# The gathers of a deformable convolution as one stream of quads: loads spread over a set, the fold behind the row sums, five broadcasts behind the fold

## The chip, the cores and the metric

The kernel runs on one core of one Trainium2 chip. The metric is the device time of one execution in microseconds. Before the change it is 5976.82 us, the median of 3 runs (5971.12 to 5979.78).

## What is computed

The reference applies four layers to an image batch x of shape 8 x 256 x 32 x 32 in float32, each with a normalisation before it and a residual behind it. The third holds three deformable convolutions, and these concern the change. Each computes offsets by a 3 x 3 convolution and then reads every pixel of every channel at its own fractional position:

```python
def _deform(x, ow, ob):
    off = _conv(x, ow, 1) + ob[None, :, None, None]
    off = off.reshape(B, C, 2, H, W)
    py = jnp.clip(yy + off[:, :, 0], 0.0, H - 1)
    px = jnp.clip(xx + off[:, :, 1], 0.0, W - 1)
    ...
    return v00 * (1 - wy) * (1 - wx) + v01 * (1 - wy) * wx + v10 * wy * (1 - wx) + v11 * wy * wx

x = x + _L0_conv_ref(_gn(x), ...)   # selective scan
x = x + _L1_conv_ref(_gn(x), ...)   # mixture of experts
x = x + _L2_conv_ref(_gn(x), ...)   # three deformable convolutions
x = x + _L3_conv_ref(_gn(x), ...)   # channel mixing
```

`_deform` runs on 256, 64 and 64 channels.

## The kernel before, in words

`kernel_program` builds the stages one after the other, each a block (or a hardware loop of blocks) with a barrier behind it: the scan layer, the expert layer, `build_offsets_1` (offsets of the first deformable convolution, 2 turns of 4 images), the constants, then `build_gather` "g1", `build_middle` 2, gather "g2", `build_middle` 3, gather "g3", and `build_last`. The stages hand data on through tensors in DRAM: `dense` (the image's second differences, called steps), `coords` (positions, y and x, in a high and a low part), `whole` (the y positions), `gathered`.

**The gather without an index.** A bilinear sample at (y, x) is a sum over all rows and columns of second differences, weighted with a clamped ramp in y and one in x. For four channels at a time (a *quad*) and half an image (512 pixels) a gather does, with n the number of the quad:

- *Broadcast* (line 1457, TensorE): a matmul with a 0/1 matrix `spread` copies a position row to 32 partitions in one of three PSUM banks, used as a ring. Each quad has five: four for x (`v`) and one for y (`k`, channel 0 of the quad). The other three y rows come by DMA (`send_rows`, line 1346), broadcast from `whole` to 32 partitions each, into `rows`, three buffers deep.
- *Read* (line 1401, ScalarE): the ramp's lower clamp, from the ring to `kw` or `vw`. It frees the bank (`ring_read`). VectorE does the same for the three sent rows (line 1423, `relu`), and GpSimd applies the upper clamp to all four (line 1415).
- *Row sums* (line 1472, TensorE): 16 matmuls on 32 x 32 tiles, image times `kw`, into four PSUM banks of one buffer only.
- *Weigh* (line 1434, VectorE): two products with `vw`, from those four banks to `prod`. It must end before the next quad's row sums start.
- *Fold* (line 1482, TensorE): four matmuls that sum 32 partitions, accumulated in one bank over the eight quads of a half. Then ScalarE copies that bank to `res` (line 1386, `evacuate`) and SyncE stores it.

A *set* is 128 channels: two halves of eight quads, 16 quads. g1 has 16 sets, g2 and g3 have 4. A hardware loop runs turns of `SETS` = 4 sets, 64 quads unrolled; coordinates and images have a buffer for each of the four sets, and semaphores are cleared between turns. The order on TensorE is written out:

```python
for n in range(-2, Q):
    tasks = turn_tasks(n)          # v, v, v of quad n+1, k of quad n+2, last v of n+1
    if n >= 0:
        rows_step(n)
    for task in tasks[:3]:
        spread_step(task)
    if n >= 1:
        fold_step(n - 1)
    for task in tasks[3:]:
        spread_step(task)
```

A broadcast waits for the read of the one three before it. ScalarE reads in the same order and evacuates behind its five reads of every eighth quad; the first fold of the next half waits for that (`res_ready`). All transfers are issued by SyncE, in program order: the first quad's rows, `load_set(0)`, two more quads' rows, `load_set(1)` to `load_set(3)`, then rows for quad n as soon as VectorE has read those of quad n-3. A `load_set` is four coordinate transfers of 512 KB (128 partitions) and four image transfers (128 KB each), which read `dense` in runs of 32 elements (128 bytes).

The producers of `dense` are `build_offsets_1` (line 1219, SyncE, in an image's first quarter) and `build_middle` (line 1638, one store per image ahead of that image's coordinates).

Of the kernel before, what the change touches and what calls it, by code (L numbers as in the profile page):

```python
# [32 lines left out]
SETS = 4  # L33
# [1115 lines left out]
def build_offsets_1(nc, t, ps, xcur, dense, coords, whole):  # L1149

    with ExitStack() as ctx:
# [54 lines left out]
        with nc.Fori(0, B // IMGS) as turn:  # L1206
            b0 = turn * IMGS
            with nc.Block() as block:

                @block.sync  # L1210
                def _(sp):
                    for m in range(2):
                        sp.dma_start(x[:, m], image(xcur, b0 + m)).then_inc(sem(f"x_loaded{m}"), 16)
                    for i, (m, k, y) in enumerate(kinds):
                        if k == 0 and y == 0:

                            sp.wait_ge(sem("steps_ready"), KC * (m + 1))
                            sp.dma_start(dense[bass.ds((b0 + m) * C, C), :].rearrange("(k p) n -> p k n", p=P),
                                         x[:, m % 2]).then_inc(sem(f"stored{m}"), 16)
                            if m + 2 < IMGS:  # L1220
                                sp.wait_ge(sem(f"stored{m}"), 16)
                                sp.dma_start(x[:, m % 2], image(xcur, b0 + m + 2)).then_inc(sem(f"x_loaded{m + 2}"), 16)
# [3 lines left out]
                        if y == 0:  # L1226
                            sp.dma_start(whole[bass.ds((b0 + m) * KC + k, 1)].rearrange("a p n -> (a p) n"),
                                         co.pos[:, i % 2, :]).then_inc(sem(f"coords_stored{i}"), 16)
                    for i, (m, k, y) in enumerate(kinds):
                        sp.wait_ge(sem(f"coords_stored{i}"), 16 * (2 - y))  # L1230
                    for m in range(IMGS):
                        sp.wait_ge(sem(f"stored{m}"), 16)
# [68 lines left out]
def build_gather(nc, ps, consts, dense, coords, whole, gathered, blocks, tag):  # L1301

    with ExitStack() as ctx:
# [6 lines left out]
        OWN = 1  # L1310
        SENT = 4 - OWN
# [4 lines left out]
        rows = st.sb("rows", [P, SB, SENT, HALF])  # L1316
        quads = [(s, j, g) for s in range(SETS) for j in range(NH) for g in range(QUADS)]
        Q = len(quads)
# [14 lines left out]
        with nc.Fori(0, blocks // SETS) as turn:  # L1333
            n0 = turn * SETS
            with nc.Block() as block:

                @block.sync
                def _(sp):
                    def send_rows(q):
                        s, j, g = quads[q]  # L1340
                        if q >= SB:
                            sp.wait_ge(sem("sent_relu"), q - SB + 1)
                        src = whole[bass.ds(n0 + s, 1), :, j * HALF:(j + 1) * HALF]\
                            .rearrange("a (r t q) n -> t (a r) q n", r=4, t=QUADS)[g]
# [4 lines left out]
                    def load_set(s):  # L1349
                        for t in range(4):  # L1350
                            sp.dma_start(coord[:, s, t, :].bitcast(F32),
                                         coords[bass.ds(n0 + s, 1)].rearrange("a y s (r t q) n -> t (a y s) r q n", r=4, t=4)[t])\
                              .then_inc(sem(f"coord_loaded{s}{t}"), 16)
                            if t == 0:
                                src = dense[bass.ds((n0 + s) * P, P), :].rearrange("(r g) (i j) -> r i g j", r=4, j=SIDE)
                                for r in range(4):
                                    sp.dma_start(img[r * SIDE:(r + 1) * SIDE, s].rearrange("p g c j -> p (g c) j"),
                                                 src[r]).then_inc(sem(f"img_loaded{s}"), 16)

                    def store(r):  # L1360
# [620 lines left out]
```

## Time and profile before

| What | Value |
|---|---|
| median of the runs | 5976.82 us |
| lowest, highest | 5971.12, 5979.78 us |
| the profiled execution, its own time | 5969.8 us |
| its span, first to last instruction | 5968.1 us |
| mean granted TensorE clock | 0.887 |
| TensorE, VectorE, ScalarE, GpSimd busy | 81%, 60%, 31%, 25% |
| moved in all | 558.13 MB, mean 94 GB/s |

All durations below are from that one execution. Busy shares are means over stages with different limits; the gathers are the stretch from about 3610 us on, interrupted by the two middle stages. "PEld" is TensorE's load of weights, "PE" its matmuls, "SPq" a transfer issued on SyncE's queue. A row with a count stands for that many like instructions in a row, with the time from the start of the first to the end of the last. A float32 matmul counts twice, since it runs in two passes. The name in brackets behind a row is what ended the engine's idle time.

### The profile page before, as it was taken

To read this page: it belongs to the slowest core of one execution; us is meant where nothing else is said; L and a number is where in the kernel's file an instruction comes from. 1 tells how busy PE (TensorE), PEld (TensorE's weight loads), DVE (VectorE), ACT (ScalarE), POOL (GpSimd) and SP (SyncE) were. 2 spreads that over 40 slices of the span, in tenths; PEclk is the share of its full clock that TensorE was granted. 3 is DMA by queue.
4 is the path that set the end of the run, shared out by engine and by line. 5 is a ranking of instruction groups with operands and counts; after the bars stand their busy time and mean duration, and the time that the engine had idled before them with its cause. 6 is when DMAs were issued, how large, how long until landed. Compare 5 with 4: busy or idle time off the path is not lost. (4 is left out here: it accounts for less than half of the span.)

```text
span 5968.1 us, 82574 instructions
## 1 busy us (share of the span) xinstructions
PE 4860.9 (81%) x30592; PEld 2689.8 (45%) x30592; DVE 3608.7 (60%) x4317; ACT 1857.1 (31%) x2899; POOL 1478.1 (25%) x1828
## 2 busy tenths in 40 slices
PE   4787887876999799979989994959596983985886
PEld 2333333324777677757767771313131332332222
DVE  6888888875666566652212223848484873863764
ACT  2222222202222122220000003848484751751660
POOL 0222222220000000011101002636363651642540
PEclk7888888867999899989999996979797996997988
DMA  1000000001000000011111119989898968978962
GB/s 30 15 20 17 21 22 21 15 21 65 15 15 8 22 15 15 8 61 74 43 71 74 53 67 193 217 180 218 178 220 181 217 171 183 218 145 143 221 178 91
DMA packets 377577, 558.13 MB, mean 94 GB/s; under 512 B 167464, under 2 KB 169064, under 8 KB 376264
## 3 DMA queue, kind: packets, MB, share of 16 engines
q1 hardware_dynamic: 377160, 552.64, 37.7%
q8 instruction: 253, 4.15, 0.3%
q14 instruction: 164, 1.34, 0.1%
HBM read 439.27 MB, written 113.25 MB: 93 GB/s over the span
## 5 line engine op out<-in xcount | busy, mean ns | idle before, releaser
L1415 POOL TENSOR_SCALAR g_kw<-g_kw 128x512 f32<-128x512 f32 x1536 | 960.8, 650 | 936.7 <-ACT g_kw L1401 637.1
L1401 ACT ACTIVATE g_vw<-ps,l_index 128x512 f32<-128x512 f32 x1536 | 971.0, 686 | 520.4 <-PE ps L1457 520.1
L1434 DVE SCALAR_TENSOR_TENSOR g_prod<-g_vw,ps 128x1024 f32<-128x1024 f32 x768 | 903.3, 1218 | 213.0 <-PE ps L1472 213.0
L1294 PE MATMUL ps<-o_pad,o_ow 128*128 128x512 f32 x3456 | 852.5, 409 | 8.5 <-DVE o_pad L822 7.7
L1457 PE MATMUL ps<-g_coord,l_spread 128*128 128x512 f32 x1920 | 678.5, 452 | 147.6 <-DMA g_coord<-coords 147.4
L1093 PE MATMUL ps<-l_pair,l_w 128*128 128x512 f32 x3072 | 780.3, 403 | 0.0
L1294 PEld LDWEIGHTS ps<-o_pad,o_ow 128*128 128x128 f32 x3456 | 657.3, 191 | 198.0 <-DVE o_pad L822 7.9
L1472 PE MATMUL ps<-g_kw,g_img 32*32 32x512 f32 x12288 | 458.9, 620 | 311.7 <-DVE g_prod L1434 272.5
L1457 PEld LDWEIGHTS ps<-g_coord,l_spread 128*128 128x128 f32 x1920 | 313.1, 194 | 831.1 <-ACT g_vw L1401 615.6
L1093 PEld LDWEIGHTS ps<-l_pair,l_w 128*128 128x128 f32 x3072 | 575.6, 191 | 156.6 <-issue 29.4
L1423 DVE TENSOR_SCALAR g_kw<-g_rows,l_index 128x1536 f32<-128x1536 f32 x384 | 389.8, 1015 | 416.0 <-DMA g_rows<-whole 416.0
L1401 ACT ACTIVATE g_kw<-ps,l_index 128x512 f32<-128x512 f32 x384 | 264.5, 689 | 1098.3 <-PE ps L1457 1081.6
L752 PE MATMUL ps<-l_rows_p,l_sel 72*128 72x512 bf16 x768 | 293.8, 473 | 211.0 <-DVE l_dbx L609 127.2
L1482 PE MATMUL ps<-g_prod,l_fold 128*32 128x512 f32 x3072 | 413.9, 611 | 9.5 <-DVE g_prod L1434 9.5
L1038 DVE TENSOR_TENSOR l_act<-ps,l_act 128x512 f32<-128x512 f32 x256 | 177.0, 691 | 398.0 <-ACT l_act L966 397.5
L428 POOL TENSOR_TENSOR l_acc<-l_acc,l_seen 128x1024 f32<-128x1024 f32 x112 | 283.2, 2528 | 512.9 <-DVE l_seen L619 512.9
L1105 PE MATMUL ps<-l_mixed,l_w 128*128 128x512 f32 x1536 | 401.3, 396 | 3.5 <-DVE l_mixed L822 1.9
L966 ACT ACTIVATE l_act<-ps 128x512 f32<-128x512 f32 x256 | 153.3, 599 | 776.1 <-PE ps L1093 776.1
L130 POOL TENSOR_TENSOR l_moments<-l_moments,l_minus_half 128x2 f32<-128x2 f32 x24 | 16.6, 692 | 1444.2 <-DVE l_moments L99 1444.2
L1105 PEld LDWEIGHTS ps<-l_mixed,l_w 128*128 128x128 f32 x1536 | 287.7, 188 | 79.0 <-issue 7.3
L1472 PEld LDWEIGHTS ps<-g_kw,g_img 32*32 32x32 f32 x12288 | 106.0, 104 | 468.6 <-POOL g_kw L1415 275.6
L1132 DVE SCALAR_TENSOR_TENSOR o_pos<-ps,o_ob,o_grid 128x1024 f32<-128x1024 f32 x32 | 41.1, 1283 | 442.2 <-PE ps L1294 441.9
(247 smaller groups left out, 4911.9 us busy)
## 6 DMA issues: line engine op xcount, KB each, us to landing
g_rows<-whole SPq DMA_DIRECT2D x1536, 192.0 KB, 4.4
g_coord<-coords SPq DMA_DIRECT2D x96, 512.0 KB, 7.2
coords<-o_parts SPq DMA_DIRECT2D x32, 1024.0 KB, 4.0
l_x<-xcur SPq DMA_DIRECT2D x16, 1024.0 KB, 6.5
coords<-o_parts SPq DMA_DIRECT2D x32, 512.0 KB, 5.1
g_img<-dense SPq DMA_DIRECT2D x96, 128.0 KB, 8.6
gathered<-g_res SPq DMA_DIRECT2D x48, 256.0 KB, 4.8
l_xn<-in_x SPq DMA_DIRECT2D x8, 1024.0 KB, 5.0
```

The costliest lines, as they stand in the source:

```text
L428: ins = nc.gpsimd.tensor_tensor(acc[:, h, :], acc[:, h, :], seen[:, i % 2, :], ALU.add)
L752: ins = nc.tensor.matmul(ps[:, lo:lo + HALF], sel[:, q, :], rows_p[:, mine, h, j * HALF:(j + 1) * HALF], start=True, stop=True)
L1093: ins = nc.tensor.matmul(bank(b_ + i % 2), w[:, a, k, e, f * P:(f + 1) * P], pair[:, m % 2, c, k, j * HALF:(j + 1) * HALF], start=(k == 0 ...
L1105: ins = nc.tensor.matmul(bank(5 + c), w2[:, a, f, e, c * P:(c + 1) * P], mixed2[:, i % 3, d, :], start=(e == 0 and f == 0 and r == 0), sto ...
L1294: ins = nc.tensor.matmul(ps[:, lo:lo + HALF], ow[:, a, kk, tap, y, k * P:(k + 1) * P], padded_rows(pad[:, m, c, kk], j, tap), start=(n == ...
L1401: nc.scalar.activation(to, bank(a % RING), ACT.Relu, bias=index[:, 0:1]).then_inc(sem("ring_read"), 1)
L1415: nc.gpsimd.tensor_scalar(part, part, 1.0, 0.0, ALU.min, ALU.max).then_inc(sem("clamped"), 1)
L1423: nc.vector.tensor_scalar(kw[:, q % KB, OWN:4, :].rearrange("p c n -> p (c n)"), rows[:, q % SB].rearrange("p c n -> p (c n)"), index[:, 0 ...
L1434: nc.vector.scalar_tensor_tensor(prod[:, n % PB, 2 * half:2 * half + 2, :].rearrange("p r n -> p (r n)"), vw[:, n % VB, 2 * half:2 * half ...
L1457: nc.tensor.matmul(bank(a % RING), spread[:, int(kind == "v"), h, c, :], coord[:, s, t, j * HALF:(j + 1) * HALF], start=True, stop=True).t ...
L1472: ins = nc.tensor.matmul(ps[c * SIDE:(c + 1) * SIDE, lo:lo + HALF], img[mine, s, g, c, :], kw[mine, n % KB, c, :], start=True, stop=True)
L1482: ins = nc.tensor.matmul(ps[r * SIDE:(r + 1) * SIDE, FOLD_BANK * HALF:(FOLD_BANK + 1) * HALF], fold[:, g, :], prod[:, n % PB, r, :], start ...
```

## The change

The gather is no longer a loop of turns but one unrolled stream of all quads of all sets (256 in g1, 64 in g2 and g3). Coordinates and images have two buffers instead of four; the loads of set s+1 are issued with the quads 7 to 11 of set s. The three sent y rows of a quad come in one transfer of 128 partitions with 1536 adjacent elements, for which `whole` is stored by halves. `dense` is laid out so that a partition of the image is one run of 4 KB, and the stores into it are scattered in runs of 32 elements instead. Of the y coordinates only those that are broadcast (16 partitions of 64) are loaded, so that a broadcast contracts over 80 partitions. On TensorE the fold comes directly behind the row sums, and all five broadcasts behind the fold.

```diff
+CROWS = 80
...
-        coord = st.sb("coord", [P, SETS, 4, N], F32R)
-        img = st.sb("img", [P, SETS, QUADS, 4, SIDE])
+        coord = st.sb("coord", [CROWS, 2, 4, N], F32R)
+        img = st.sb("img", [P, 2, QUADS, 4, SIDE])
...
-        quads = [(s, j, g) for s in range(SETS) for j in range(NH) for g in range(QUADS)]
+        quads = [(s, j, g) for s in range(sets) for j in range(NH) for g in range(QUADS)]
...
-        with nc.Fori(0, blocks // SETS) as turn:
...
-                        for r in range(4):
-                            sp.dma_start(rows[r * SIDE:(r + 1) * SIDE, q % SB],
-                                         src[r, OWN:4].partition_broadcast(SIDE)).then_inc(sem(f"rows_sent{q % SB}"), 16)
+                sp.dma_start(rows[:, q % SB].rearrange("p c n -> p (c n)"),
+                                 src.unsqueeze(1).to_broadcast([4, SIDE, 3 * HALF])).then_inc(sem(f"rows_sent{q % SB}"), 16)
...
+                def load_image(s):
+                    if s >= 2:
+                        sp.wait_ge(sem("rows_summed"), PER_SET * (s - 1))
+                    sp.dma_start(img[:, s % 2].rearrange("p g c j -> p (g c j)"),
+                                 dense[s].rearrange("i (r g) j -> r i (g j)", r=4)).then_inc(sem(f"img_loaded{s % 2}"), 16)
+
+                def load_coords(s, t):
+                    at_x = coords[s, 1].rearrange("s (r t q) n -> t s r q n", r=4, t=4)[t]
+                    at_y = coords[s, 0].rearrange("s (r t h q) n -> t q s r h n", r=4, t=4, h=2)[t, 0]
+                    sp.dma_start(coord[0:CM, s % 2, t, :].bitcast(F32), at_x).then_inc(sem(f"coord_loaded{s % 2}{t}"), 16)
+                    sp.dma_start(coord[CM:CROWS, s % 2, t, :].bitcast(F32), at_y).then_inc(sem(f"coord_loaded{s % 2}{t}"), 16)
...
+                for q in range(SB, Q):
+                    send_rows(q)
+                    s, part = divmod(q, PER_SET)
+                    if s + 1 < sets:
+                        if part == 7:
+                            load_image(s + 1)
+                        if 8 <= part < 12:
+                            load_coords(s + 1, part - 8)
+                    if q % QUADS == SB + 2 and q >= QUADS:
+                        store(q // QUADS - 1)
...
-                        for task in tasks[:3]:
-                            spread_step(task)
-                        if n >= 1:
-                            fold_step(n - 1)
-                        for task in tasks[3:]:
-                            spread_step(task)
+                    if n >= 1:
+                        fold_step(n - 1)
+                    for task in tasks:
+                        spread_step(task)
...
-                        sp.dma_start(dense[bass.ds(b * CM, CM), :], step[:, m, :]).then_inc(sem("stored"), 16)
+                        part = slice(m % 2 * CM, (m % 2 + 1) * CM)
+                        sp.dma_start(dense[bass.ds(turn * (PASS // 2) + m // 2, 1), :, part, :].rearrange("a i p j -> (a p) i j"),
+                                     step[:, m, :].rearrange("p (i j) -> p i j", j=SIDE)).then_inc(sem("stored"), 16)
...
-        dense = dram("dense", (B * C, N))
+        dense = dram("dense", (B * C // P, SIDE, P, SIDE))
...
-        whole = dram("whole", (B * C // P, P, N))
+        whole = dram("whole", (B * C // P, NH, P, HALF))
```

`build_offsets_1` stores `dense` in the same scattered way, in two transfers per image instead of one.

How the instructions stand on TensorE in the middle of a gather, before (1472 row sums, 1457 broadcasts, 1482 fold):

```order
L1472 MATMUL ps<-g_kw,g_img 32x512 x16
L1457 MATMUL ps<-g_coord,l_spread 128x512 x3
L1482 MATMUL ps<-g_prod,l_fold 32x512 x4
L1457 MATMUL ps<-g_coord,l_spread 128x512 x2
L1472 MATMUL ps<-g_kw,g_img 32x512 x16
```

and in the changed kernel, where the same steps have the lines 1476, 1461 and 1486:

```order
L1476 MATMUL ps<-g_kw,g_img 32x512 x16
L1486 MATMUL ps<-g_prod,l_fold 32x512 x4
L1461 MATMUL ps<-g_coord,l_spread 128x512 x5
L1476 MATMUL ps<-g_kw,g_img 32x512 x16
L1486 MATMUL ps<-g_prod,l_fold 32x512 x4
```

The fold no longer lies between the third and the fourth broadcast: five follow each other.

On SyncE's queue, the first transfers of a gather before (`ISA` is address arithmetic; rows of one quad, a quarter of the coordinates, the image):

```order
L1346 DMA g_rows<-whole 32x3x512
L1351 ISA
L1351 DMA g_coord<-coords 128x1x1024
L1357 ISA
L1357 DMA g_img<-dense 32x32x32
```

and in the changed kernel, from the gather's first transfer to the first ones of set 1:

```order
L1342 DMA g_rows<-whole 128x1x1536
L1354 DMA g_coord<-coords 64x1x1024
L1355 DMA g_coord<-coords 16x1x1024
L1348 DMA g_img<-dense 128x1x1024
L1342 DMA g_rows<-whole 128x1x1536 x2
...
L1342 DMA g_rows<-whole 128x1x1536 x5
L1348 DMA g_img<-dense 128x1x1024
L1342 DMA g_rows<-whole 128x1x1536
```

Four row transfers per quad became one, the image is one transfer of whole rows instead of four in short runs, and the second set's image is asked for behind the rows of the eighth quad instead of ahead of those of the fourth.

## Rows read from the trace of the kernel before

**Rows 1.** The page's first line.
```profile
span 5968.1 us, 82574 instructions
```

**Rows 2.** Line 1472 in each gather: instruction count, ns min/median/max, first and last start.
```profile
L1472 PE MATMUL ps<-g_kw,g_img x8192: 584/588/1058, 3622.3 to 4864.4; 32*32 32x512 f32 x200
...
L1472 PE MATMUL ps<-g_kw,g_img x2048: 584/588/1058, 5016.8 to 5308.4; 32*32 32x512 f32 x187
...
L1472 PE MATMUL ps<-g_kw,g_img x2048: 584/588/1058, 5485.9 to 5776.6; 32*32 32x512 f32 x187
```

**Rows 3.** Stretches: us, busy us per engine (instructions), granted clock, DMA share, GB/s.
```profile
core 0: us, PE busy (x) PEld busy (x) DVE busy (x) ACT busy (x) POOL busy (x), PEclk, DMA share, GB/s
3610.00:3680.00 70.00, 17.95 (x133) 6.24 (x133) 9.98 (x10) 12.81 (x21) 8.84 (x16) 0.55 1.08 208
3740.00:3900.00 160.00, 155.70 (x1889) 51.12 (x1890) 137.46 (x126) 132.84 (x215) 105.82 (x168) 1.00 0.92 217
```

**Rows 4.** Timeline of one quad: start us, us, engine, line, operation, count, [idle before].
```profile
3743.84 0.27 PEld L1472 LDWEIGHTS ps<-g_kw,g_img 32*32 32x32 f32 x32 [0.51 <-issue]
...
3744.96 0.53 PEld L1457 LDWEIGHTS ps<-g_coord,l_spread 128*128 128x128 f32 x3 [0.84 <-ACT g_vw L1401]
...
3745.19 2.35 DVE L1434 SCALAR_TENSOR_TENSOR g_prod<-g_vw,ps 128x1024 f32<-128x1024 f32 x2 [0.53 <-PE ps L1472]
...
3745.49 1.85 ACT L1401 ACTIVATE g_vw<-ps,l_index 128x512 f32<-128x512 f32 x3 [0.65 <-PE ps L1457]
...
3745.85 0.16 PEld L1482 LDWEIGHTS ps<-g_prod,l_fold 128*32 128x32 f32 x8 [0.37 <-issue]
...
3746.85 0.30 PEld L1457 LDWEIGHTS ps<-g_coord,l_spread 128*128 128x128 f32 x2 [0.84 <-ACT g_vw L1401]
...
3747.66 0.27 PEld L1472 LDWEIGHTS ps<-g_kw,g_img 32*32 32x32 f32 x32 [0.51 <-issue]
```

**Rows 5.** Timeline, first broadcasts of the first gather.
```profile
3619.03 0.69 ACT L1401 ACTIVATE g_kw<-ps,l_index 128x512 f32<-128x512 f32 x1 [947.12 <-PE ps L1457]
...
3619.77 0.29 PEld L1457 LDWEIGHTS ps<-g_coord,l_spread 128*128 128x128 f32 x1 [0.65 <-ACT g_kw L1401]
...
3624.25 2.95 PE L1457 MATMUL ps<-g_coord,l_spread 128*128 128x512 f32 x5
```

**Rows 6.** Timeline, last quads of the first turn, on TensorE.
```profile
3911.94 0.27 PEld L1472 LDWEIGHTS ps<-g_kw,g_img 32*32 32x32 f32 x32 [0.63 <-issue]
...
3913.05 0.16 PEld L1482 LDWEIGHTS ps<-g_prod,l_fold 128*32 128x32 f32 x8 [0.84 <-issue]
```

**Rows 7.** Timeline, one copy of the fold bank on ScalarE.
```profile
3706.56 0.60 ACT L1386 ACTIVATE g_res<-ps 128x512 f32<-128x512 f32 x1
```

**Rows 8.** Timeline, beginning of the first turn.
```profile
3610.10 1.88 SPq L1346 DMA_DIRECT2D g_rows<-whole  x4
...
3636.05 2.02 PE L1472 MATMUL ps<-g_kw,g_img 32*32 32x512 f32 x32 [8.85 <-DVE g_prod L1434]
...
3639.58 1.73 PE L1482 MATMUL ps<-g_prod,l_fold 128*32 128x512 f32 x8
...
3677.70 1.02 DVE L1423 TENSOR_SCALAR g_kw<-g_rows,l_index 128x1536 f32<-128x1536 f32 x1 [37.10 <-DMA g_rows<-whole]
```

**Rows 9.** Timeline of SyncE, last stores of a middle stage's turn.
```profile
4926.56 2.03 SPq L1638 DMA_DIRECT2D dense<-o_step  x1
...
4929.99 1.45 SPq L1642 DMA_DIRECT2D coords<-o_parts  x2
```

**Rows 10.** Timeline, one quarter in the offsets stage.
```profile
3518.72 1.28 DVE L1132 SCALAR_TENSOR_TENSOR o_pos<-ps,o_ob,o_grid 128x1024 f32<-128x1024 f32 x1 [22.34 <-PE ps L1294]
```

**Rows 11.** DMA issues: count, KB each, median us from issue to landing.
```profile
g_rows<-whole SPq DMA_DIRECT2D x1536, 192.0 KB, 4.4
...
g_img<-dense SPq DMA_DIRECT2D x96, 128.0 KB, 8.6
...
dense<-o_step SPq DMA_DIRECT2D x16, 256.0 KB, 5.1
```

More of the change, by code:

```diff
@@ L1449, in spread_step @@
                         kind, q, c = task
                         a = at[task]
-                        s, j, g = quads[q]
-                        t, h = divmod(g, 2)
-                        if a >= RING:
-                            pe.wait_ge(sem("ring_read"), a - RING + 1)
-                        if j == 0 and h == 0:
-                            pe.wait_ge(sem(f"coord_loaded{s}{t}"), 16)
-                        nc.tensor.matmul(bank(a % RING), spread[:, int(kind == "v"), h, c, :],
-                                         coord[:, s, t, j * HALF:(j + 1) * HALF], start=True,
-                                         stop=True).then_inc(sem("ring_filled"), 1)
@@ L1461, in rows_step @@
-                    def rows_step(n):
-                        s, j, g = quads[n]
-                        if j == 0 and g == 0:
-                            pe.wait_ge(sem(f"img_loaded{s}"), 64)
-                        pe.wait_ge(sem("clamped"), 4 * (n + 1))
-                        if n:
-                            pe.wait_ge(sem("weighted"), 2 * n)
-                        for c in range(4):
-                            for r in range(4):
-                                mine = slice(r * SIDE, (r + 1) * SIDE)
-                                lo = (ROW_BANK + r) * HALF
-                                ins = nc.tensor.matmul(ps[c * SIDE:(c + 1) * SIDE, lo:lo + HALF], img[mine, s, g, c, :],
-                                                       kw[mine, n % KB, c, :], start=True, stop=True)
-                        ins.then_inc(sem("rows_summed"), 1)
@@ L1476, in fold_step @@
-                    def fold_step(n):
-                        s, j, g = quads[n]
-                        pe.wait_ge(sem("weighted"), 2 * (n + 1))
-                        if g == 0 and n:
-                            pe.wait_ge(sem("res_ready"), n // QUADS)
-                        for r in range(4):
-                            ins = nc.tensor.matmul(ps[r * SIDE:(r + 1) * SIDE, FOLD_BANK * HALF:(FOLD_BANK + 1) * HALF],
-                                                   fold[:, g, :], prod[:, n % PB, r, :], start=(g == 0), stop=(g == QUADS - 1))
-                        ins.then_inc(sem("folded"), 1)
@@ new lines, in _ @@
+                    if n >= QUADS and n % QUADS == 0:
+                        evacuate(n // QUADS - 1)
+                evacuate(sets * NH - 1)
+            @block.gpsimd
+            def _(pool):
+                for q in range(Q):
+                    for c in range(4):
+                        if c == 0:
+                            pool.wait_ge(sem("ring_read"), at["k", q, 0] + 1)
+                        else:
+                            pool.wait_ge(sem("sent_relu"), q + 1)
+                        part = kw[:, q % KB, c, :]
+                        nc.gpsimd.tensor_scalar(part, part, 1.0, 0.0, ALU.min, ALU.max).then_inc(sem("clamped"), 1)
```

265 lines of the change are left out of this document (134 added, 131 removed).

## The prediction

> **What bounds the kernel now.** I started from the span, 5968.1 us [rows 1], and asked which part of it the change can reach: nearly only the three gathers. The row sums (TensorE line 1472) date them: they run from 3622.3 to 4864.4, from 5016.8 to 5308.4 and from 5485.9 to 5776.6 us [rows 2], 1242.1 + 291.6 + 290.7 = 1824.4 us in all, for 256, 64 and 64 quads. Each turn also begins with about 12.2 us between the first transfer at 3610.10 [rows 8] and the first row sums at 3622.3 [rows 2]; taken for all three gathers that is 36.6 us, and 1861.0 us together.
>
> The stretch from 3740 to 3900 us is the steady state: granted clock 1.00 (2.4 GHz) and 126 instructions of VectorE, three per quad [rows 3], so 42 quads in 160 us, 3.81 us each. 384 quads at that pace are 1463 us, so some 400 us of the gathers go into the beginnings of turns. There the granted clock is 0.55 on average, near the lower level (1.2 GHz), the DMA share is full, and VectorE waits up to 37.10 us for rows to land [rows 3, 8]: SyncE asks for all four sets of coordinates and images before the fourth quad's rows.
>
> The timeline of one period [rows 4] shows the loop that sets 3.82 us. VectorE weighs for 2.35 us from 3745.19 to 3747.54; 0.12 us later, at 3747.66, TensorE starts the next row sums; 1.35 us after their start (3743.84 to 3745.19) VectorE may weigh again. 2.35 + 0.12 + 1.35 = 3.82. TensorE's own list is nearly as long: row sums to broadcasts 1.12, three broadcasts 0.89, fold 1.00, two broadcasts 0.81, again 3.82, with hardly any slack.
>
> **The change, part by part.** *Removed turn beginnings (gain).* With one stream per gather and the next set's loads spread over quads 7 to 11 of a set, the 400 us mostly vanish. What remains is three starts. Before the first row sums 768 + 320 + 512 KB must land; at 217 GB/s [rows 3] that is 7.5 us, and with ScalarE and GpSimd behind it I take 10 us instead of 12.2. The fourth quad's rows land after 4 x 768 + 1280 + 512 KB, 23 us, and are clamped at about 27 us, where a steady stream would be at 23.4; two quads at the lower clock add 4 us. So a start costs 10 + 8 = 18 us, three 54 us (bounds 36, if the transfers keep ahead, and 100, if each still loses a 20 us wait).
>
> *New order on TensorE (loss).* Behind the row sums now stands the fold, then five broadcasts in a row through a ring of three banks. The fourth waits until ScalarE has read the first, the fifth for the second; before, the fold lay between and hid exactly this. Step by step, in starts of weight loads: row sums to fold 3913.05 - 3911.94 = 1.11 us [rows 6]; fold to first broadcast 3746.85 - 3745.85 = 1.00 [rows 4]; broadcast to ScalarE's read 3745.49 - 3744.96 = 0.53, a read 0.69, and two reads (1.85 - 0.69) / 2 = 0.58 apart [rows 4, 5]; a freed bank to the next broadcast 0.05 (3619.03 + 0.69 against 3619.77 [rows 5]). So the fourth starts 0.53 + 0.69 + 0.05 = 1.27 after the first, the fifth at 1.85. From the fifth to the next row sums I have bounds: 0.30, the pitch of broadcasts in a group, and 0.81 - 0.30 = 0.51 from the pair before the row sums [rows 4]; that pair's gap includes VectorE's wait, so I take 0.43. The period is 1.11 + 1.00 + 1.85 + 0.43 = 4.39 us. It exceeds the 3.82 us of the VectorE loop, which gets slack, so TensorE and ScalarE's ring become the bound.
>
> *The evacuation behind them.* Every eighth quad ScalarE also copies the fold bank, 0.60 us [rows 7], after its five reads. Counted from the row sums, its first read starts at 1.11 + 1.00 + 0.53 = 2.64, the fourth when the third is done, 4.39, the fifth at 4.97, and the copy lasts from 5.56 to 6.16. The next fold was due at 4.39 + 1.11 = 5.50 and must wait for the copy: 0.7 us per eight quads, 0.09 per quad. Before, the fold came 2 us behind the row sums and missed it. Mean period 4.48 us, bounds 4.30 and 4.62. 381 intervals give 1707 us; with 54 us for starts the gathers take 1761 instead of 1861: **-100 us**.
>
> *Transfers in the gather.* A set now moves 16 x 768 KB of rows, 1280 of coordinates (512 KB per quarter before, 320 now), 512 of image and 512 stored: 14.94 MB per 71.7 us, 208 GB/s, against 217 GB/s carried at a share of 0.92 [rows 3]. Row pieces grow from 2 to 6 KB, and one DMA takes the place of four of 192 KB. So the transfers stay hidden, narrowly: with TensorE at 3.82 us they would need 244 GB/s, and the old order would have met that limit instead. SyncE's one queue carries them; its extra issues at quads 7 to 11 put 5.8 MB into five periods (22.4 us, 258 GB/s), some 4 us late against rows that are asked for three quads ahead. I take nothing, and as a bound 2 us at each of the 21 changes of set (42 us), if that lead is too short.
>
> *Scattered stores of the image.* The steps are now written in runs of 128 bytes. In the offsets stage they are issued in the first quarter of an image, with TensorE the bound (VectorE idles 22.34 us per quarter for it [rows 10]): nothing. In the two middle stages the last of four stores is issued at 4926.56 for 2.03 us, 3.4 us ahead of the last coordinates [rows 9], so a little is exposed at the end of four turns. The nearest rows are the 128 KB image loads, also 128-byte runs, with 8.6 us to landing [rows 11]. Bounds 0 and 8.6 us per turn; I take 2, as three of the four stores lie under other work: **+8 us**. The Trainium skill ("DMA: Bandwidth & Descriptors", its opening table) holds that transfers under 512 B are read-modify-write; no run here shows a store of that kind yet. If that doubled the 5.1 us in which these stores land now [rows 11], the term would be 4 x 5.1, about 20 us, an estimate by that page, and the total 12 us later.
>
> *The rest.* The broadcast constants shrink from 128 x 2048 to 80 x 1280 elements, loaded and cast once: -2 us at most, I take -2. The contraction over 80 instead of 128 rows leaves the columns that stream as they were: nothing.
>
> The sum is -100 + 8 - 2 = -94 us on the profiled execution's 5969.8 us: 5876. The median of the runs, 5976.8, lies 7 us above it, so I say **5883 us**, 1.6% faster.
>
> **The rivals.** (1) *The transfers become the bound.* If large broadcast pieces move more slowly than small ones did, each period is set by landing. The break-even is 94 / 381 = 0.25 us more per quad, 4.73 us, or 198 GB/s. For it: at the first turn's start, with mixed loads, the fabric gave 208 GB/s at a full share; the margin over the need is nil by that row. Against it: that row is full of 128-byte pieces, which the change takes out. At 190 GB/s a quad takes 4.91 us, +164 us: 6047 us, slower than before. (2) *The clock falls.* TensorE now idles briefly in front of the fourth and fifth broadcasts. At the lower level a quad is 2.02 for row sums, 1.73 for the fold [rows 8], 2.95 for five broadcasts [rows 5], 6.7 us; all gathers so would cost +846 us, 6729 us, and 11% of them at that level would eat the gain. Against it: the idle is about a sixth of the period, in pieces of 0.3 to 0.4 us, and at the lower clock TensorE has no idle at all, after which the rows show it risen. The Trainium skill ("TensorE: Matmul & The Clock Gate", "A second HAM failure mode: psum-queue depth-cycling") describes this very pattern, a tensor engine that idles briefly while it cycles through banks and swings between its levels; no stretch of this trace does so in steady state. (3) *The ring costs less than I count*, because the fifth broadcast's bank is free sooner or the next row sums start beside it. Then VectorE's 3.82 us or the transfers' limit, about 236 GB/s by 217 / 0.92, sets the pace: 14.94 MB in 63.3 us, 4.0 us a quad, another 183 us less: 5700 us. Against it: every link of the chain is a row.
>
> **How the numbers follow.** Forecast 77%, rival 1 11%, rival 2 4%, rival 3 8%. The forecast's own range, from a period of 4.30 to 4.62 (-69 to +53) and starts and stores on top, is 5815 to 5945. To hold 8 in 10 I reach a little toward both sides, 5795 to 5950; most of rival 3, rival 2 and the far part of rival 1 stay out. A measurement of this kernel tells about 0.2%, 12 us, from no change. Faster by more than that: the forecast nearly whole and rival 3, 84%; within it 4%, the near edge of rival 1; slower 12%.
>
> **What would show it.** In the changed profile's steady state: row sums every 4.39 us with one of 5.1 in eight; weight loads of the fourth and fifth broadcasts waiting for ScalarE in each quad; the fold waiting for the copy once per eight; VectorE idle 1.1 us per quad in front of the weighing; no wait of VectorE for rows outside the first few quads of a gather; granted clock 1.00 and a DMA share near 0.88. A first row sum about 10 us after a gather's first transfer and about 1150 us for the first gather's row sums would confirm the starts. I am wrong if the period is near 3.9 (rival 3), if VectorE waits for rows in every quad (rival 1), or if broadcasts take turns at two durations (rival 2).

## The result and the profile after

| What | Before | After |
|---|---|---|
| median of 4 runs each | 5976.25 us | 7404.62 us |
| lowest, highest | 5971.12, 5979.78 | 7388.99, 7419.44 |
| the profiled execution, its own time | 5969.8 | 7388.99 |
| mean granted TensorE clock | 0.887 | 0.777 |

The changed kernel takes 1.2391 times as long (95% interval 1.2362 to 1.2419), where 0.984 was forecast. The page's first line, against [rows 1]:

```profile
span 7387.0 us, 78774 instructions
```

The row sums of the three gathers, now line 1476, against [rows 2] (count, ns min/median/max, first and last start):

```profile
L1476 PE MATMUL ps<-g_kw,g_img x8192: 584/1056/1058, 3636.0 to 5793.5; 32*32 32x512 f32 x200
...
L1476 PE MATMUL ps<-g_kw,g_img x2048: 584/1056/1058, 5953.6 to 6483.9; 32*32 32x512 f32 x187
...
L1476 PE MATMUL ps<-g_kw,g_img x2048: 584/1056/1058, 6671.1 to 7197.3; 32*32 32x512 f32 x187
```

2157.5 + 530.3 + 526.2 = 3214.0 us instead of 1824.4: 1389.6 of the span's 1418.9 us more lie between the first and the last row sums of a gather. The median matmul went from 588 to 1056 ns: most ran at the lower of the two clock levels. What VectorE waits for says why. First the kernel before, then the changed one (us in total, times, longest):

```profile
DVE g_kw L1423 <- DMA g_rows<-whole: 416.0, 30, 38.9
```

```profile
DVE g_kw L1427 <- DMA g_rows<-whole: 2030.5, 384, 24.2
```

Before, 30 of 384 quads waited for their rows; now all do. But no bandwidth is used up. A stretch in the middle of the first gather, columns as in [rows 3]:

```profile
4000.00:4400.00 400.00, 282.23 (x2117) 76.31 (x2117) 156.81 (x144) 146.46 (x246) 112.28 (x191) 0.66 0.28 112
```

48 quads in 400 us, 8.3 each, at 112 GB/s and a DMA share of 0.28, where before had 217 GB/s and 0.92 [rows 3]. The transfers are late and the DMA engines idle. A view of the DMA over 8 us, each digit the busy share of the 16 engines in 0.2 us (2 is 20 to 29%, 9 is 90% or more), with the GB/s beneath, resolves this:

```profile
DMA  2222122279994422222222221322222222222212
GB/s 92 123 123 123 61 92 123 92 276 430 338 348 133 174 102 123 123 92 92 92 123 92 123 123 61 123 92 123 92 123 123 92 92 92 123 92 123 123 61 123
```

While rows are sent, the share stands at 2, which fits 4 engines of 16. The only digits of 9 are a `gathered` store. The single pieces in the trace say the same: in this stretch exactly four of 6144 bytes are under way for 7.6 of the 8 us, and each takes 0.235 us. A quad's 128 pieces over 4 engines are 32 x 0.235 = 7.5 us, and that is the period, one quad in the timeline:

```profile
4201.87 1.02 DVE L1427 TENSOR_SCALAR g_kw<-g_rows,l_index 128x1536 f32<-128x1536 f32 x1 [4.33 <-DMA g_rows<-whole]
...
4209.36 1.02 DVE L1427 TENSOR_SCALAR g_kw<-g_rows,l_index 128x1536 f32<-128x1536 f32 x1 [4.21 <-DMA g_rows<-whole]
```

7.49 us from one to the next, 4.21 of it VectorE's wait for rows. The transfer of a quad is one DMA of four source rows, each repeated 32 times: its slowest dimension has size 4, where before each of four transfers had 32. That was the theory to test. The Trainium skill ("DMA: Bandwidth & Descriptors", section "Why a DMA increments its semaphore by 16 and not by 1") has it as a rule: a DMA runs on the largest number of engines up to 16 that divides the slowest dimension of both its sides, on the lowest-numbered ones. By that rule this transfer gets 4 engines, which fits the digits.

The trace lets one count it, too. Besides the data it has packets of 4 bytes, and their number in the first gather fits one per transfer and engine: 2624 in the changed kernel are 256 transfers of rows x 4, 16 of the image x 4, 128 of coordinates x 8 and 32 stores x 16.

Not all of the excess is this: averaged by a quad's place in its set, eleven of the sixteen periods are 7.5 to 8.2 us, but quad 7 takes 12.6 and 8 to 11 take 9.1 to 9.7. There the next set's image and coordinates are loaded.

### The profile page after: what moved, and what is told of

It reads as the page before. It is cut to its first block and busy times, and to the rows that moved or that the text cites. A ratio compares the mean times of both kernels' runs of the same rounds, so it can differ in the third digit from the quotient of the medians.

```text
span 7387.0 us, 78774 instructions
## 1 busy us (share of the span) xinstructions
PE 5717.2 (77%) x30544; PEld 2841.5 (38%) x30592; DVE 3604.9 (49%) x4317; ACT 1815.4 (25%) x2899; POOL 1422.3 (19%) x1828
## 5 line engine op out<-in xcount | busy, mean ns | idle before, releaser
L1419 POOL TENSOR_SCALAR g_kw<-g_kw 128x512 f32<-128x512 f32 x1536 | 904.8, 615 | 2408.7 <-DVE g_kw L1427 2253.5
L1476 PE MATMUL ps<-g_kw,g_img 32*32 32x512 f32 x12288 | 748.1, 1012 | 791.6 <-DVE g_prod L1438 787.0
L1461 PE MATMUL ps<-g_coord,l_spread 80*128 80x512 f32 x1920 | 919.1, 569 | 244.3 <-DMA g_coord<-coords 155.8
L1461 PEld LDWEIGHTS ps<-g_coord,l_spread 80*128 80x128 f32 x1920 | 431.0, 246 | 1188.0 <-issue 643.0
L1486 PE MATMUL ps<-g_prod,l_fold 128*32 128x512 f32 x3072 | 705.4, 1012 | 1.9 <-DVE g_prod L1438 1.9
L1486 PEld LDWEIGHTS ps<-g_prod,l_fold 128*32 128x32 f32 x3072 | 76.9, 139 | 615.0 <-issue 607.9
L613 DVE TENSOR_TENSOR_SCAN l_states<-ps,l_dbx 128x1024 f32<-128x1024 f32 x128 | 293.2, 2290 | 23.6 <-PE ps L752 19.6
```

The lines of the kernel that those rows point to most:

```text
L613: nc.vector.tensor_tensor_scan(states[:, i % 2, :], ps[:, 0:2 * HALF], dbx[:, i % 2, :], 0.0, ALU.mult, ALU.add).then_inc(sem("da_used"), 1)
L1419: nc.gpsimd.tensor_scalar(part, part, 1.0, 0.0, ALU.min, ALU.max).then_inc(sem("clamped"), 1)
L1461: nc.tensor.matmul(bank(a % RING), spread[:, h, c if kind == "v" else 4, :], coord[:, s % 2, t, j * HALF:(j + 1) * HALF], start=True, stop ...
L1476: ins = nc.tensor.matmul(ps[c * SIDE:(c + 1) * SIDE, lo:lo + HALF], img[mine, s % 2, g, c, :], kw[mine, n % KB, c, :], start=True, stop=True)
L1486: ins = nc.tensor.matmul(ps[r * SIDE:(r + 1) * SIDE, FOLD_BANK * HALF:(FOLD_BANK + 1) * HALF], fold[:, g, :], prod[:, n % PB, r, :], start ...
```

## The experiments

The times are medians, with lowest and highest; the ratio is to the kernel before on the same chip, with its 95% interval. "Period by place" is the mean time from one quad's row sums to the next quad's, over sets 1 to 15 of the first gather, worked out from the starts in the trace; places count from 0.

### Rows in four transfers, in the new and in the old order (e1, e2)

```diff
-                    sp.dma_start(rows[:, q % SB].rearrange("p c n -> p (c n)"),
-                                 src.unsqueeze(1).to_broadcast([4, SIDE, 3 * HALF])).then_inc(sem(f"rows_sent{q % SB}"), 16)
+                    for r in range(4):
+                        sp.dma_start(rows[r * SIDE:(r + 1) * SIDE, q % SB].rearrange("p c n -> p (c n)"),
+                                     src[r].partition_broadcast(SIDE)).then_inc(sem(f"rows_sent{q % SB}"), 16)
```

e2 has this too, and the order of before on TensorE:

```diff
+                    for task in tasks[:3]:
+                        spread_step(task)
                     if n >= 1:
                         fold_step(n - 1)
-                    for task in tasks:
+                    for task in tasks[3:]:
                         spread_step(task)
```

> The changed kernel, but each quad's sent rows go in four transfers of 32 partitions again (still one run of 6 KB per partition), new order on TensorE kept. Theory (the single transfer has 4 as its slowest dimension and runs on 4 of the 16 DMA engines): the wait of VectorE for rows goes away, the DMA share in the steady state rises above 0.45, the quads are then set by TensorE and the ring of banks, 4.4 us with one of 5.1 in eight, and the kernel takes about 5870 us (5820 to 5950). Rival (6 KB pieces, or broadcasts from one row, are slow as such): quads stay above 7 us and the time above 7000 us.

> As e1, and the fold back between the third and the fourth broadcast. If the new order costs what the prediction says (ring of three banks, copy of the fold bank), quads fall to 3.82 us, VectorE's loop, and the time to about 5640 us (5600 to 5720), some 0.6 us x 384 = 230 us below e1. If the order costs nothing, e1 and e2 agree within 20 us. If transfers bind at 217 to 236 GB/s, as the prediction's third rival has it, quads take 4.0 us and the time is 5700 us or more.

e1: 6122.71 us (6108.54 to 6140.19), 1.0238 (1.0208 to 1.0268). e2: 6113.94 us (6090.39 to 6144.67), 1.0243 (1.0201 to 1.0285). Splitting the one transfer takes 1282 of the 1428 us of excess away; the pieces are still 6 KB, so it isn't their size. The stretch of 400 us in e1, with a DMA share of 0.82 instead of 0.28:

```profile
4000.00:4400.00 400.00, 344.39 (x3571) 105.93 (x3555) 259.66 (x237) 241.90 (x406) 188.24 (x316) 0.90 0.82 186
```

But both stay above before, and the totals expected were far too low. The quads away from the set's loads go as expected: 4.37 us with 5.17 in one of eight in e1, 3.82 in e2. The excess sits at places 7 to 11: 8.0, 6.35, 5.95, 5.64, 5.47 us in e1 and 10.79, 6.48, 6.12, 5.68, 5.67 in e2. VectorE there in e2, place 7 first:

```profile
4083.05 1.01 DVE L1428 TENSOR_SCALAR g_kw<-g_rows,l_index 128x1536 f32<-128x1536 f32 x1
...
4095.11 1.02 DVE L1428 TENSOR_SCALAR g_kw<-g_rows,l_index 128x1536 f32<-128x1536 f32 x1 [8.16 <-DMA g_rows<-whole]
...
4100.96 1.02 DVE L1428 TENSOR_SCALAR g_kw<-g_rows,l_index 128x1536 f32<-128x1536 f32 x1 [2.57 <-DMA g_rows<-whole]
```

and SyncE before it:

```profile
4074.39 0.57 SPq L1349 DMA_DIRECT2D g_img<-dense  x1
4076.46 1.71 SPq L1343 DMA_DIRECT2D g_rows<-whole  x4
```

VectorE waits 8.16 us for the rows issued right behind the image (512 KB, slowest dimension 4). Hence the next suspects.

### The new order alone, in the kernel before (e3)

The kernel before, with this alone:

```diff
-                        for task in tasks[:3]:
-                            spread_step(task)
                         if n >= 1:
                             fold_step(n - 1)
-                        for task in tasks[3:]:
+                        for task in tasks:
                             spread_step(task)
```

> The kernel before with the new order on TensorE alone: turns, transfers and layouts as before. If the ring theory is right, a quad in steady state takes 4.4 us and each eighth 5.1, mean 4.48 instead of 3.82; in the quads behind each turn's beginning that is about 360 x 0.66 = 240 us, so 6215 us (6150 to 6260). Rival (VectorE's loop goes on hiding it): 5976 us within 15.

6201.56 us (6195.56 to 6209.90), 1.0369 (1.0352 to 1.0386): +222 us for the order, as expected. The chain of the prediction stands in the weight loads, here around a copy of the fold bank:

```profile
4071.96 0.23 PEld L1472 LDWEIGHTS ps<-g_kw,g_img 32*32 32x32 f32 x32 [0.24 <-issue]
4073.03 0.17 PEld L1482 LDWEIGHTS ps<-g_prod,l_fold 128*32 128x32 f32 x8 [0.84 <-issue]
4074.05 0.53 PEld L1457 LDWEIGHTS ps<-g_coord,l_spread 128*128 128x128 f32 x3 [0.84 <-ACT g_vw L1401]
4075.32 0.19 PEld L1457 LDWEIGHTS ps<-g_coord,l_spread 128*128 128x128 f32 x1 [0.75 <-ACT g_vw L1401]
4075.90 0.19 PEld L1457 LDWEIGHTS ps<-g_coord,l_spread 128*128 128x128 f32 x1 [0.40 <-ACT g_vw L1401]
4076.33 0.23 PEld L1472 LDWEIGHTS ps<-g_kw,g_img 32*32 32x32 f32 x32 [0.24 <-issue]
4077.45 0.62 ACT L1386 ACTIVATE g_res<-ps 128x512 f32<-128x512 f32 x1
4078.18 0.19 PEld L1482 LDWEIGHTS ps<-g_prod,l_fold 128*32 128x32 f32 x8 [1.62 <-issue]
...
4081.50 0.23 PEld L1472 LDWEIGHTS ps<-g_kw,g_img 32*32 32x32 f32 x32 [0.25 <-issue]
```

Row sums to fold 1.07, fold to broadcasts 1.02. The fourth and the fifth broadcast wait for ScalarE and start 1.27 and 1.85 us after the first, as predicted. Row sums to row sums 4.37 (4.39 predicted); with the copy, whose end at 4078.07 the fold waits for, 5.17 (5.1 predicted).

### Rows in two transfers, slowest dimension 2 (e4)

```diff
-                    for r in range(4):
-                        sp.dma_start(rows[r * SIDE:(r + 1) * SIDE, q % SB].rearrange("p c n -> p (c n)"),
-                                     src[r].partition_broadcast(SIDE)).then_inc(sem(f"rows_sent{q % SB}"), 16)
+                    for r in range(2):
+                        sp.dma_start(rows[r * CM:(r + 1) * CM, q % SB].rearrange("p c n -> p (c n)"),
+                                     src[2 * r:2 * r + 2].unsqueeze(1).to_broadcast([2, SIDE, 3 * HALF])).then_inc(sem(f"rows_sent{q % SB}"), 16)
```

> The changed kernel with each quad's rows in two transfers of 64 partitions, slowest dimension 2. Theory (as many DMA engines as the slowest dimension): both run on the same 2 engines, 64 pieces of 0.235 us each, 15 us per quad, so about 4170 us outside the gathers + 384 x 16 = 10300 us (9900 to 10700), DMA share near 0.14. Rival (one large transfer is slow, smaller ones are better): 7400 us or less.

10275.04 us (10272.21 to 10277.88), 1.7186 (1.7150 to 1.7222), and 15.0 us per plain quad. This is the run that tells the theories apart: the transfers are smaller and twice as many, and the period doubles with the slowest dimension halved. The view of 8 us again:

```profile
DMA  1100111110011111001114100111149981110011
GB/s 61 61 31 31 61 61 61 61 61 31 31 61 61 61 61 61 31 31 61 61 61 143 61 31 31 61 61 61 61 184 399 399 338 72 61 61 31 31 61 61
```

While rows alone move, the digit is 1 (12.5% is two engines) or falls to 0, at 31 to 61 GB/s; in the changed kernel it was 2 at 123.

### The image in four transfers (e5)

```diff
-                    sp.dma_start(img[:, s % 2].rearrange("p g c j -> p (g c j)"),
-                                 dense[s].rearrange("i (r g) j -> r i (g j)", r=4)).then_inc(sem(f"img_loaded{s % 2}"), 16)
+                    for r in range(4):
+                        sp.dma_start(img[r * SIDE:(r + 1) * SIDE, s % 2].rearrange("p g c j -> p (g c j)"),
+                                     dense[s].rearrange("i (r g) j -> r i (g j)", r=4)[r]).then_inc(sem(f"img_loaded{s % 2}"), 16)
```

> As e2 (rows in four transfers, old order on TensorE), and the image too in four transfers of 32 partitions. In e2 the plain quads take 3.82 us, but the quads in which the next set is loaded 5.7 to 10.8 us. Theory: the image (slowest dimension 4) and the coordinates (2) run on the first 4 and 2 DMA engines, and the rows behind them, which need all 16, wait in those engines' queues. Then the first of these quads (10.8 us) shrinks to about 6 us, the other five stay, and the time falls by 24 x 5 = 100 us against e2, to about 6010 us. Rival (the fabric as a whole is short by the bytes of the loads): no change, 6114 us within 20.

5947.12 us (5931.52 to 5948.54), 0.9951 (0.9932 to 0.9970), 167 us below e2, more than the 100 expected, and now below before by 0.5%. Place 7 went from 10.79 to 3.82 us, where I had expected about 6. That settles what held it: the image in a single transfer kept the rows behind it waiting. Places 8 to 15 still take 4.89, 6.77, 6.32, 6.01, 5.26, 4.76, 4.54 and 4.21 us, with the coordinates next to them.

### The coordinates in 16 small transfers, in both orders (e6, e7)

```diff
+                        sp.dma_start(coord[u * 8:(u + 1) * 8, s % 2, :, :].bitcast(F32), at_x)\
+                          .then_inc(sem(f"coord_all{s % 2}"), 16)
...
+                    sp.dma_start(coord[CM + 2 * u:CM + 2 * u + 2, s % 2, :, :].bitcast(F32), at_y)\
+                      .then_inc(sem(f"coord_all{s % 2}"), 16)
...
-                            load_coords(s + 1, part - 8)
+                            load_part(s + 1, part - 8)
+                            load_y(s + 1, 2 * (part - 8))
+                            load_y(s + 1, 2 * (part - 8) + 1)
```

e6 is e5 with this; e7 has the new order beside it.

> As e5, and the coordinates of every set but the first in transfers of 8 partitions (x, slowest dimension 8) and 2 (y). Theory: the long quads go, what stays is the fabric's limit. With e2's loaded stretches at about 230 GB/s a set of 14.94 MB needs 65 us, 4.06 us per quad, so about 5770 us (5710 to 5850), below the kernel before. Rival (the fabric's bytes already bind in e2): 6010 us or more, as e5.

> As e6 with the new order on TensorE: the change as the prediction had it, with transfers that are spread over the engines. Quads of 4.37 us with one of 5.17 in eight, mean 4.47, need 209 GB/s, below the fabric's limit, so the transfers are hidden and the time is about 5920 us (5870 to 5970): 150 us above e6 and 0.9% below the kernel before.

e6: 6172.48 us (6156.64 to 6175.45), 1.0330 (1.0309 to 1.0351). e7: 6227.37 us (6207.33 to 6248.81), 1.0417 (1.0395 to 1.0439). Both misses, 225 us worse than e5 for e6. I had read the coordinates' slowest dimension as the 2 of the high and low parts. In the pieces of e5's trace the x coordinates ran eight at a time: the dimensions of 2 and 4 lie at one stride and count as 8. The same holds for y by the 4-byte packets of e5's first gather: 18944 are 16 for each of the 1120 transfers of rows, image and stores, and 8 for each of the 128 of coordinates. My split left x on eight engines and, by the same count in e6 (19183, one short of what that gives), put y on two; places 8 to 11 take 7.86, 9.76, 7.97 and 7.77 us. The edit also makes a set's first broadcast wait for all of its coordinates instead of a quarter; places 14 and 15, where that would show, take 4.54 and 4.40 us, in e5 4.54 and 4.21.

### Without the loads of later sets (e8)

```diff
-                    if s + 1 < sets:
+                    if s == 0:
```

> As e2, but coordinates and image are loaded for the first two sets of each gather only; the later sets compute on those (left out: the transfers of the later sets, so their results are of other data). Theory: without these loads all quads take 3.82 us, and the time is about 5670 us (5640 to 5720), a lower bound for one stream with the old order. Rival (something in the stream other than these loads stretches those quads, the rows alone or instruction fetch): above 5900 us.

5729.24 us (5718.83 to 5737.64), 0.9593 (0.9574 to 0.9612), 9 us above the range expected; the three starts take 22.0 to 23.2 us each here, as the first image is still one transfer. Without the set loads 247 of 255 periods of the first gather are 3.82 us, in a stream of 16 x 768 KB per set. The stretch:

```profile
4000.00:4400.00 400.00, 388.16 (x4725) 127.19 (x4723) 344.04 (x316) 332.43 (x538) 265.26 (x420) 1.00 0.89 216
```

So row transfers of 6 KB pieces on 16 engines keep up with the fastest loop, at 216 GB/s. The set loads, their volume and their shape, are the 385 us between e2 and this.

### The set loads spread over eleven quads, in both orders (e9, e10)

```diff
-                        if part == 7:
-                            load_image(s + 1)
-                        if 8 <= part < 12:
-                            load_coords(s + 1, part - 8)
+                        if 5 <= part < 9:
+                            load_strip(s + 1, part - 5)
+                        if 8 <= part < 16:
+                            load_half(s + 1, (part - 8) // 2, (part - 8) % 2)
```

A strip is one of e5's four image transfers; a half is one half of a quarter's x coordinates, y with the first. e9 has the old order, e10 the new one: e10 is the change with the forecast's order and its transfers put right, but it also spreads the loads over more quads than the change does.

> As e5 (rows and image in transfers of 32 partitions, old order), with the next set's loads spread over more quads: one image strip with each of quads 5 to 8, half of a quarter's x coordinates with each of quads 8 to 15. Theory: the x coordinates (slowest dimension 8 after merging) load the first 8 DMA engines only; per set these carry 128 row pieces of 0.40 us and about 12 us of other pieces, 64 us, 4.0 to 4.1 us per quad if nothing is bunched. So about 5750 us (5700 to 5830), below e5 by 100 us or more and below the kernel before. Rival (bunching is not what costs): 5945 us within 20.

> As e9 with the new order on TensorE. This is what the prediction thought it was costing. Quads of 4.37 us with one of 5.17 in eight (mean 4.47) need less than the engines can carry, so the order sets the pace: about 5910 us (5870 to 5960), some 160 us above e9. Rival (with one stream, transfers bind either way): e9 and e10 within 30 us.

e9: 5893.65 us (5872.22 to 5915.57), 0.9852 (0.9830 to 0.9874). e10: 5906.11 us (5897.25 to 5912.46), 0.9880 (0.9864 to 0.9897). Both are below before, by 1.5% and 1.2%, clear of the interval. e10 came as expected, with 4.37 and 5.17 us; e9 was expected at 5750 (5700 to 5830), a miss, and is level with e10: their runs overlap, and the row sums' spans sum to 1753.1 us in e9 and 1745.7 in e10. The two lie within the 30 us that e10's rival had named, yet not for its reason, as transfers don't bind in e10 (below). The new order costs 0.55 us a quad, and taking it out (e9) gives nothing back. e9's periods show where it went. VectorE in one set:

```profile
4072.64 1.02 DVE L1444 TENSOR_SCALAR g_kw<-g_rows,l_index 128x1536 f32<-128x1536 f32 x1 [1.73 <-DMA g_rows<-whole]
4077.97 1.02 DVE L1444 TENSOR_SCALAR g_kw<-g_rows,l_index 128x1536 f32<-128x1536 f32 x1 [2.04 <-DMA g_rows<-whole]
...
4091.55 1.01 DVE L1444 TENSOR_SCALAR g_kw<-g_rows,l_index 128x1536 f32<-128x1536 f32 x1
4098.09 1.01 DVE L1444 TENSOR_SCALAR g_kw<-g_rows,l_index 128x1536 f32<-128x1536 f32 x1
4104.62 1.01 DVE L1444 TENSOR_SCALAR g_kw<-g_rows,l_index 128x1536 f32<-128x1536 f32 x1
```

and the stretches of the waits and of what follows them:

```profile
4058.00:4084.00 26.00, 19.34 (x226) 6.42 (x225) 18.17 (x17) 16.03 (x27) 12.53 (x22) 0.97 0.86 204
4086.00:4118.00 32.00, 32.00 (x226) 9.00 (x225) 15.97 (x16) 16.04 (x26) 11.74 (x20) 0.50 0.71 170
```

While the set's loads pass, the 3.82 us loop waits for rows (4.2 to 5.8 us a quad), and TensorE is busy 19.34 of 26 us, idle in pieces of 0.9 to 1.6 us. Then the granted clock is 0.50 (1.2 GHz) for the next 32 us, TensorE is busy without a gap, and quads without any wait take 6.53 us. Of e9's 255 periods in the first gather (by VectorE's steps on the sent rows) 95 end in a wait for rows (mean 5.15 us); of the others 121 are below 3.95 us, most of them 3.82, 18 are about 6.53, and 21 lie between. Over 255 x 3.82 us that makes 195 us more: 127 in the periods with a wait, 68 in the others. e10 has 184 us more, but from its longer loop: only 27 of its periods end in a wait, and one is at the lower level. The same stretch of 400 us:

```profile
4000.00:4400.00 400.00, 366.86 (x3942) 115.34 (x3926) 289.68 (x263) 276.94 (x448) 215.62 (x351) 0.88 0.89 206
```

```profile
4000.00:4400.00 400.00, 356.23 (x4030) 113.08 (x4015) 294.57 (x269) 272.83 (x457) 212.69 (x359) 1.00 0.90 211
```

e9 (first) moves no more than e10, with clock 0.88 against 1.00.

### The kernel before with rows of slowest dimension 4, and the change with the old order (e11, e12)

e11 leaves everything as before but groups a quad's row transfers by channel (three of 128 partitions) instead of by row (four of 32):

```diff
-                        for r in range(4):
-                            sp.dma_start(rows[r * SIDE:(r + 1) * SIDE, q % SB],
-                                         src[r, OWN:4].partition_broadcast(SIDE)).then_inc(sem(f"rows_sent{q % SB}"), 16)
+                        for c in range(SENT):
+                            sp.dma_start(rows[:, q % SB, c], src[:, OWN + c].unsqueeze(1).to_broadcast([4, SIDE, HALF]))\
+                              .then_inc(sem(f"rows_sent{q % SB}"), 16)
```

e12 is the changed kernel with e2's order.

> The kernel before with one edit: a quad's sent rows go in three transfers of 128 partitions (slowest source dimension 4) in place of four of 32; same bytes, same 2 KB pieces, fewer transfers. Theory (4 of 16 engines): 96 pieces per engine of about 0.084 us each, 8.1 us per quad, so 4144 us outside the row sums + 384 x 8.3 + six turn beginnings of 50 us = 7600 us (7300 to 7900). Rival (fewer, larger transfers are no worse): 5970 us.

> The changed kernel with the fold back between the broadcasts and nothing else undone. Quads are set by the rows' landing, 7.5 us, so the order costs nothing: 7400 us within 60. Rival (the order has a share in the loss on the record): 7250 us or less.

e11: 7556.96 us (7549.52 to 7564.39), 1.2648 (1.2622 to 1.2673), with 7.8 us per quad away from the turns' beginnings. Its stretch of 400 us, which has a turn's beginning in it:

```profile
4000.00:4400.00 400.00, 209.70 (x1851) 64.09 (x1847) 137.21 (x126) 132.12 (x214) 97.81 (x167) 0.74 0.36 112
```

The loss appears in the old kernel, turns, order, 2 KB pieces and all, with the grouping alone. e12: 7405.89 us (7402.29 to 7409.49), 1.2395 (1.2370 to 1.2420), level with the changed kernel: under the limit of 4 engines the order costs nothing. Its granted clock in that stretch is 0.51, where the changed kernel has 0.66, and the time is the same.

## Why the prediction was wrong

5883 us was forecast, 7404.62 measured, outside the range of 5795 to 5950.

**The step that failed** is the one on transfers in the gather: "one DMA takes the place of four of 192 KB. So the transfers stay hidden, narrowly". I compared bytes with GB/s [rows 3] and pieces with pieces, and took for granted that any transfer has all 16 engines. The rate of [rows 3] was reached by transfers whose slowest dimension was 32 or more. The term set at nothing is 7404.62 - 6122.71 = 1282 us by e1 against the changed kernel, confirmed from the other side by e11 and in size by e4. The page of the Trainium skill cited above states the rule, and I had drawn on that page for the stores only.

**The bound beside it,** 42 us for the changes of set if the lead is too short, was too small, mostly for the same reason: e1, in the order that it was made for, lies 217 us above e10, some 29 of them in the three starts. In the old order, against e2, the image alone was 167 us (e5), the spreading of the rest 53 more (e9), and 164 remain to e8, which leaves those transfers out.

**The order** was right. 4.37 and 5.17 us were measured for 4.39 and 5.1, and the rows of e3 show the steps. What I hadn't seen is that the order's cost depends on the transfers: +222 us in the kernel before (e3), but 9 against e2 (e1), 12 against e9 (e10) and nothing under the 4 engines (e12), all three within the spread of the runs.

**The forecast's mechanism otherwise.** e10 gives 1154.7 us for the first gather's row sums where the text said about 1150, and 5906 us in all, inside the range, with a DMA share of 0.90 where it said 0.88. That is no success of the forecast, as that kernel isn't the change; it says the other terms were about right in sum.

**The starts.** I took 10 us from a gather's first transfer to its row sums. In the changed kernel it was 21.4, 19.7 and 20.0 us: rows, coordinates and image, none on more than 8 engines, must land first. The first transfer (SyncE's issue; the first row sums are at 3636.0):

```profile
3614.65 0.64 SPq L1342 DMA_DIRECT2D g_rows<-whole  x1
```

With the rows alone in four transfers it was 23.2 us (e2), with the image in four too 13.3 (e5), so the image's single transfer is what held them. The order doesn't matter here: it is 13.3 us in e10 as well, still 1 more than before.

**The stores in runs of 128 bytes** were to cost 8 us. From the last row sums of a gather to the first transfer of the next, the middle stages with their stores take 140.4 and 167.2 us, before 140.2 and 165.2: 2.2 us together. Over all runs, with either kind of stores, these stretches vary from 138.4 to 141.5 and from 161.8 to 167.3 us, so no cost shows above that. Nor does the doubling that I had put at about 20 us, my estimate from the opening table of the Trainium skill's page ("DMA: Bandwidth & Descriptors"); the stores were not tried by themselves. Median landing of these stores in the middle stages, against [rows 11]:

```profile
dense<-o_step SPq DMA_DIRECT2D x16, 256.0 KB, 6.1
```

**The constants** (-2 us) can't be judged by themselves: the gather's first transfer came at 3614.65 instead of 3610.10 us [rows 8], and in e3, whose stages ahead of it are those of before, at 3620.01. So stages that no edit touches vary by more than this term, and than any cost of the scattered stores in the offsets stage, which I had put at nothing.

**The rivals.** Rival 1 was right in kind (VectorE waits for rows in each quad, as it said it would), wrong in mechanism and price: 112 GB/s instead of 190, a limit by engines and not by the fabric. Its break-even of 4.73 us was passed by 2.8 us in every quad. Rival 2, the falling clock, did occur, but as a follower: TensorE, idle for want of rows, ran at 0.66; without the waits (e8) it ran at 1.00, and at 0.51 (e12) the time was no longer. In e9 it costs time of its own, 18 periods x 2.7 = 49 us in the first gather. Rival 3 fell: the ring costs what I counted. I had given 11% to rival 1 and none to anything above 6047 us except rival 2.

**Open.** How much of the 164 us between e9 and e8 goes with the volume of the set loads and how much with the coordinates' eight engines, or with e9's x pieces of 2 KB instead of 4, wasn't tried. Nor was the new layout of the image alone.

## What to carry to other kernels

Read the shape of each DMA, not only its bytes: merging several transfers into one can put a small dimension outermost and confine it to that many engines, and a view of DMA share beside the wait (late transfers at a share of 0.28) tells this from a full fabric. A narrow transfer can also hold back wide ones that are issued after it (e2 against e5). Price a slower order only together with the resource beside it: where transfers set the pace its cost vanishes (e12), and a loop that runs ahead of its data can lose to waits and the clock what it gains (e9 against e10).

## What the hardware showed that I hadn't expected

- Rows of one quad (128 pieces of 6144 bytes, 768 KB) took 7.5 us with slowest dimension 4 and 15.0 us with 2, and with 32 less than the 3.82 us of the loop.
- A 6144-byte broadcast piece took 0.235 us with four engines at work and 0.40 to 0.43 us with all sixteen (e9): per engine 26 and about 15 GB/s. Sixteen engines carried 217 GB/s in the steady stretch of before [rows 3] and 216 in e8, four 104 GB/s with rows alone.
- A 512 KB transfer of slowest dimension 4 delayed rows on 16 engines that were issued 2 us later: 10.79 instead of 3.82 us for that quad. The Trainium skill's rule cited above has such a DMA on the lowest-numbered engines, which would make the rows share them; which engines they were, no view here shows.
- Dimensions of 2 and 4 at one stride counted as 8: the coordinates' pieces and packets in e5.
- The 4-byte packets of a gather gave the number of engines per transfer away: 2624 in the changed kernel, 18944 in e5.
- After 26 us in which TensorE idled a quarter of the time, never longer than 1.6 us at once, the granted clock was 0.50 for 32 us though TensorE had no gap in them (e9).
